# Graph layer with experts: GpSimd splits the expert weights in pieces of 256 columns, padding columns filled behind the first expert's rows

## The chip, the cores and the metric

One core of one Trainium2 chip runs the kernel. The metric is the device time of one execution in microseconds (us), lower is better; three executions are given as their median with the lowest and the highest. One further execution was profiled, and all rows below are from that one.

## What is computed

The reference takes 6250 nodes with 256 features and 206250 edges sorted by target node:

```python
xn = _layernorm(x)
x = x + edge_attention(xn) + mixer(xn)          # graph attention over the edges, and a linear attention
h = _layernorm(x)                               # from here on: the expert part
logits = h @ gate_w + gate_b                    # 8 experts
idx = argmax(softmax(logits)); prb = its probability
C = ceil(1.25 * T / E)                          # 977 rows of capacity for each expert
buf[e, pos] = h                                 # a row goes to its expert's next free slot, if pos < C
hmid = relu(buf @ w1[e] + b1[e])                # 977 x 256 by 256 x 1024
ybuf = hmid @ w2[e] + b2[e]                     # 977 x 1024 by 1024 x 256
x = x + ybuf[idx, pos] * prb * kept
```

All of it is in 32-bit floats.

## The kernel before

The first 2,706 us of the profiled execution are the edge attention and the mixer, which the change leaves alone. Then come the second layer norm with the routing, and the experts.

**Routing** (lines 1380 to 1590). The rows go by in seven groups of seven tiles. VectorE takes the statistics, ScalarE the square root and the centering, TensorE the transposes and the gate's product, VectorE the argmax and the slots (`route`), and GpSimd scatters each tile of rows into the DRAM buffer `hb_d` with one indirect DMA (L1473, 49 of them). Before these scatters GpSimd's queue holds `split_w(0, 0)`, the split of the first expert's `w1`.

**Splitting.** TensorE multiplies in a rounded 32-bit form, so every operand x is kept as two parts: `hi`, a copy of x in that form (L1544), and `lo = x - hi` (L1545). A product is then three products: hi by hi, hi by lo, lo by hi (`product`, L129 in the profile). The function `split` writes both parts with whichever engine it is given. VectorE splits the rows after their transposition, straight out of PSUM, 512 columns at a time. GpSimd splits the weights in `split_w(e, i)`: i = 0 is `w1` (128 partitions by 2048 columns), i = 1 is `w2` (the same size), with one copy and one subtraction of 2048 columns each, and a wait between them.

**Experts** (lines 1607 to 1690). For each expert e, in this order on each engine's queue:

- GpSimd: `split_w(e, 1)`, as soon as `w2` is there and the scatters of the expert before are through its queue.
- TensorE, first product: 8 blocks f of 128 hidden columns, each in two column groups of 490 and 488 rows with 6 matmuls for each, 96 in all. ScalarE writes each group twice with bias and ReLU (L1645): to `hf[f % 2]`, a plain copy in one of two buffers, and to `hh`, the hi part. VectorE then writes `hl = hf - hh` over 978 columns (L1647). ScalarE's block f waits for VectorE's block f-2, since `hf` has two buffers.
- TensorE: `turn(e+1, 0)`, the transposes (L1615) of half of the next expert's rows. VectorE splits them (L1544, L1545).
- GpSimd: `split_w(e + 1, 0)`, which waits until the first product of e has read `w1`.
- TensorE, second product: waits for `split_w(e, 1)`. Eight row tiles j, each over the 8 blocks f with 3 matmuls of 256 columns, 192 in all. Block f waits for its L1647. After two pairs of tiles lies `turn(e+1, 1)`.
- For each pair of tiles VectorE adds the bias out of PSUM (L1670), ScalarE scales (L1674), VectorE replaces infinities and NaN (L1678 to L1683), and GpSimd issues two indirect DMAs that add to the output (L1686).

**Padding.** `hh` and `hl` have 1024 columns for each block, of which L1647 and L1645 write 978. The 46 others are zeroed once, ahead of the first `turn(0, 0)`: a memset of `hf[0]` (L1602) and two copies of 368 columns (L1605) into `hh` and `hl`, on VectorE.

```python
        def split_w(e, i):
            w, hi, lo, used = ((w1r, w1h, w1l, t_l1), (w2r, w2h, w2l, t_l2))[i]
            wait(G, t_wl[i][e], used.get(e - 1))
            t_ws[i][e] = split(G, g, hi, lo, w)
...
        t_pad = v(V.memset(hf[0], 0.0))
...
        turn(0, 0)
        turn(0, 1)
```

Of the kernel before, what the change touches and what calls it, by code (L numbers as in the profile page):

```python
# [14 lines left out]
CP = 1024  # L15
CE = 978
# [16 lines left out]
class Sem:  # L33
# [6 lines left out]
    def inc(self, ins, k=1):  # L40
        ins.then_inc(self.h, k)
        self.n += k
        return (self, self.n)
# [19 lines left out]
def gps_layer_kernel(nc, x, src, dst, wall, ball, wmix, wqm, wout, wo, bo, b_out, gate_w, gate_b, w1, b1, w2, b2, out):  # L63
    f32 = mybir.dt.float32
# [4 lines left out]
    ALU = mybir.AluOpType  # L69
    ACT = mybir.ActivationFunctionType  # L70
    AX = mybir.AxisListType
    V, S, T, G, Y = nc.vector, nc.scalar, nc.tensor, nc.gpsimd, nc.sync

    ctx = ExitStack()
    with ctx:
# [15 lines left out]
        def take(n):  # L91
            top[0] += n
            assert top[0] <= 53008 - WIDE, top[0]
            return A[:, top[0] - n:top[0]]

        def r3(ap, b):
            return ap.rearrange("p (a b) -> p a b", b=b)
# [14 lines left out]
        wait = Waits()  # L112

        def v(ins):
            return sv.inc(ins)

        def a(ins):
            return sa.inc(ins)

        def g(ins):  # L120
            return sg.inc(ins)
# [4 lines left out]
        def product(o, pairs, first=True, last=True):  # L126

            for i, (l, r) in enumerate(pairs):
                m = T.matmul(o, l, r, start=(first and i == 0), stop=(last and i == len(pairs) - 1))  # L129
            return m  # L130


        R0 = take(12544)
# [164 lines left out]
        def norm(xt, n, o=None):  # L298
# [4 lines left out]
            for i in range(n):  # L303
# [8 lines left out]
        quot, hi, lo, over = [R1[:, 16 * i:16 * i + NB13] for i in range(4)]  # L312
# [5 lines left out]
        t = v(V.tensor_copy(firsts, fi_i))  # L318
        wait(V, t)
        t = v(V.tensor_scalar(out=quot, in0=firsts, scalar1=0.5, scalar2=1.0 / NT, op0=ALU.add, op1=ALU.mult))  # L320
        wait(V, t)
        t = v(V.tensor_copy(hi_i, quot))
        wait(V, t)
        t = v(V.tensor_copy(hi, hi_i))
        wait(V, t)
        t = v(V.tensor_tensor(over, hi, quot, ALU.is_gt))
        wait(V, t)
        t = v(V.tensor_tensor(hi, hi, over, ALU.subtract))
        wait(V, t)
        t = v(V.scalar_tensor_tensor(out=lo, in0=hi, scalar=-float(NT), in1=firsts, op0=ALU.mult, op1=ALU.add))  # L330
        v(V.tensor_tensor(oneH, iota.unsqueeze(1).to_broadcast([128, NB13, 128]), hi.unsqueeze(2).to_broadcast([128, NB13, 128]), ALU.is_equal))
        wait(V, t)
        t = v(V.tensor_tensor(oneL, iota[:, 0:NT].unsqueeze(1).to_broadcast([128, NB13, NT]),
                              lo.unsqueeze(2).to_broadcast([128, NB13, NT]), ALU.is_equal))
# [4 lines left out]
        t = v(V.memset(cnt[:, 0:1], 0.0))  # L339
        wait(V, t_hist)  # L340
        t = v(V.tensor_copy(cnt[:, 1:50], ps[5][:, 0:NT]))
        wait(V, t)
        t = v(V.tensor_tensor_scan(R1[:, 1280:1330], cnt, cnt, 0.0, ALU.add, ALU.bypass))
# [3 lines left out]
        t = v(V.tensor_copy(below, ps[5][:, 64:65]))  # L347
# [316 lines left out]
        t = a(S.activation(bh, bal, ACT.Copy))  # L664
# [4 lines left out]
        t = v(V.tensor_scalar(out=bh0, in0=bh.bitcast(f32), scalar1=e0, scalar2=None, op0=ALU.mult))  # L669
# [40 lines left out]
        for grp in range(7):  # L710
            for j in range(7):
                t = grp * 7 + j
# [33 lines left out]
                for u in tiles:  # L746
# [14 lines left out]
                    if 16 <= u < 32:  # L761
                        i = u - 16
# [101 lines left out]
        t = v(V.memset(dsb, 0.0))  # L864
        wait(V, t, t_dt[NT - 1])
        for h in range(4):
            for q in range(2):
                t = v(V.tensor_copy(dsb[q * 64:(q + 1) * 64, h, q * 64:(q + 1) * 64], dts[h][q * 64:(q + 1) * 64, q * 64:(q + 1) * 64]))
# [3 lines left out]
        t = sp.inc(m)  # L872
        wait(V, t)
        for h in range(4):
            t = v(V.tensor_copy(T1[:, h, :], ps[h][:, 0:256]))
# [4 lines left out]
        t = sp.inc(m)  # L880
# [595 lines left out]
        t_sc = [None]  # L1476
# [33 lines left out]
        def out_group(grp):  # L1510
            wait(Y, t_x2[grp])
            if grp < 6:
                return dma(Y, out[grp * 896:(grp + 1) * 896, :].rearrange("(t p) d -> p t d", p=128), XH[:, grp * 7:grp * 7 + 7, 0:256], s_o)
            dma(Y, out[grp * 896:grp * 896 + 768, :].rearrange("(t p) d -> p t d", p=128), XH[:, 42:48, 0:256], s_o)
            return dma(Y, out[48 * 128:N, :], XH[0:N - 48 * 128, 48, 0:256], s_o)
# [5 lines left out]
        w1r, w2r = r3(R0[:, 0:2048], 1024), r3(R0[:, 2048:4096], 256)  # L1521
        b1_s = R0[:, 4096:4160]
        b2_s = R0[:, 4160:6208]
        hf = [R0[:, 6208 + CE * i:6208 + CE * (i + 1)] for i in range(2)]
        yv = [R0[:, o:o + 512] for o in (8192, 8704, 11272, 11784)]
        t_yq = {}
        u1, u2 = R0[:, 9216:9728], R0[:, 9728:10240]
        rowb = [[z.rearrange("p (j w) -> p j w", w=HR) for z in p] for p in
                ((R3[:, 0:1032], R3[:, 1032:2064]), (R0[:, 10240:11272], IDX[:, 0:1032]))]
        hh, hl = [r3(HL[:, 8192 * i:8192 * (i + 1)], 1024) for i in range(2)]  # L1530
        xh, xl = [r3(HL[:, 16384 + 2048 * i:16384 + 2048 * (i + 1)], 1024) for i in range(2)]
        w2h, w2l = [r3(HL[:, 20480 + 2048 * i:20480 + 2048 * (i + 1)], 256) for i in range(2)]
        w1h, w1l = [r3(HL[:, 25344 + 2048 * i:25344 + 2048 * (i + 1)], 1024) for i in range(2)]
        s_we = [sem("s_we0"), sem("s_we1")]
        t_l1, t_l2, t_xp, t_xc, t_y = {}, {}, {}, {}, {}
        t_wl, t_ws = ({}, {}), ({}, {})

        def load_w(e, i):
            wait(Y, t_ws[i].get(e - 1))
            t_wl[i][e] = dma(Y, (w1r, w2r)[i], kpart((w1, w2)[i][e]), s_we[i])  # L1540

        def split(eng, inc, hi, lo, x):

            wait(eng, inc(eng.tensor_copy(hi, x)))  # L1544
            return inc(eng.tensor_tensor(lo, x, hi.bitcast(f32), ALU.subtract))  # L1545

        def split_w(e, i):
            w, hi, lo, used = ((w1r, w1h, w1l, t_l1), (w2r, w2h, w2l, t_l2))[i]
            wait(G, t_wl[i][e], used.get(e - 1))
            t_ws[i][e] = split(G, g, hi, lo, w)  # L1550

        wait(Y, t_fin)
        load_w(0, 0)
        wait(G, t_fin)
        split_w(0, 0)
        t_nm = {0: scale2(0, root2(0, spread2(0)))}
        for s_ in range(NT + 3):
            grp, i = divmod(s_, 7)
            if i == 0 and grp < 7:
                t_o = out_group(grp)  # L1560
# [22 lines left out]
        t_sc = t_sc[0]  # L1583
# [14 lines left out]
        load_w(0, 1)  # L1598
        t_rl = {0: load_r(0), 1: load_r(1)}
        load_w(1, 0)  # L1600
        wait(V, t_sc, t_o)
        t_pad = v(V.memset(hf[0], 0.0))  # L1602
        wait(V, t_pad)
        for z in (hh, hl):
            v(V.tensor_copy(z[:, :, CE:CP], r3(hf[0][:, 0:8 * (CP - CE)], CP - CE)))  # L1605
        bank_free = {}

        def turn(e, jj):

            wait(T, t_rl[e][jj])  # L1610
            for k in range(2):
                b = ps[k]
                wait(T, bank_free.get(k))
                for j in range(4):
                    m = T.transpose(b[:, j * 128:(j + 1) * 128], rowb[e % 2][jj][:, j, k * 128:(k + 1) * 128], ident)  # L1615
                t_xp[e] = sp.inc(m)
                wait(V, t_xp[e], t_l1.get(e - 1))
                bank_free[k] = split(V, v, *[z[:, k, jj * 512:(jj + 1) * 512] for z in (xh, xl)], b[:, :])
            t_xc[e] = bank_free[1]

        COLS = [(0, 490), (490, 488)]
        turn(0, 0)
        turn(0, 1)
        t_hs = {}
        wait(S, t_bb, t_sc, t_o)
        wait(V, t_bb)
        wait(G, t_o, t_sc)
        for e in range(8):
            split_w(e, 1)
            if e > 0 and e + 1 < 8:  # L1630
                load_w(e + 1, 0)
# [4 lines left out]
            for f in range(8):  # L1636
                for n, (c0, cw) in enumerate(COLS):
                    i = 2 + (f * 2 + n) % 4
                    wait(T, bank_free.get(i))
                    fs, cs = slice(f * 128, (f + 1) * 128), slice(c0, c0 + cw)  # L1640
                    t = sp.inc(product(ps[i][:, 0:cw], [(l[:, k, fs], r[:, k, cs]) for k in range(2)
                                                        for l, r in ((w1h, xh), (w1h, xl), (w1l, xh))]))
# [6 lines left out]
            if e + 1 < 8:  # L1649
                turn(e + 1, 0)  # L1650
                split_w(e + 1, 0)
            wait(T, t_ws[1][e])
            for j in range(0, 8, 2):
                rows_ = rowb[e % 2][j // 4]
                jr = j % 4
                i = 6 + j // 2 % 2
# [16 lines left out]
                for jj in (j, j + 1):  # L1673
                    t = a(S.activation(y[:, (jj - j) * 256:(jj - j + 1) * 256], y[:, (jj - j) * 256:(jj - j + 1) * 256], ACT.Copy,  # L1674
                                       scale=rows_[:, jj % 4, 257:258]))
# [3 lines left out]
                t = v(V.tensor_scalar(out=u2, in0=y, scalar1=0.0, scalar2=-1e4, op0=ALU.is_lt, op1=ALU.mult))  # L1679
# [3 lines left out]
                t = v(V.copy_predicated(y, u2.bitcast(i32), u1))  # L1683
# [39 lines left out]
```

## Time and profile before

| | |
|---|---|
| Median of 3 runs | 3256.96 us (3250.91 to 3258.57) |
| Profiled execution | 3256.88 us, of which the span of its records is 3255.3 us |
| VectorE busy | 2563.4 us (79%) |
| TensorE busy | 2218.1 us (68%) |
| GpSimd busy | 2073.9 us (64%) |
| ScalarE busy | 709.9 us (22%) |
| Routing and second norm | 2706 to 2811 us of the span |
| Experts | 2811 to 3254 us of the span |

How to read it: the profile records each instruction with its start, its length, the line of the kernel it comes from and the shapes it wrote and read. PE is TensorE (PEld its loads of weights), DVE VectorE, ACT ScalarE, POOL GpSimd, SP the queue that issues most DMAs. In square brackets stands how long the engine was idle ahead of the instruction, and whose completion ended that. An instruction's length includes time in which it had started and could not proceed. PEclk is the clock granted to TensorE, as a share of 2.4 GHz.

### The profile page before, as it was taken

The numbers are of one execution on the slowest core, as the hardware profiler recorded it, in microseconds if no ns is written. First come the engines' busy times: TensorE is split into PE (matmuls) and PEld (weight loads), VectorE is DVE, ScalarE is ACT, GpSimd is POOL, SyncE is SP. The second block draws the span as 40 slices with busy tenths as digits, with TensorE's granted clock in tenths as the row PEclk, the third lists the DMA queues.
The fourth block names the chain that finished last, engine by engine and source line by source line (L and its number), as shares of the span: only waits on it lengthen the run. The fifth ranks groups of instructions, "written<-read, shape, count | busy, mean of one in ns | idle before, by whom it ended". The sixth has DMA issues, their size and how long they took to land. (4 is left out here: it accounts for less than half of the span.)

```text
span 3255.3 us, 36410 instructions
## 1 busy us (share of the span) xinstructions
PE 2218.1 (68%) x9298; PEld 1743.9 (54%) x9299; DVE 2563.4 (79%) x3578; ACT 709.9 (22%) x2051; POOL 2073.9 (64%) x1996
## 2 busy tenths in 40 slices
PE   6896996778785566555655565655555545698988
PEld 4674775556564444443444443444444425587877
DVE  4555767888899899898989898988989854477675
ACT  3442551111111011111111111111111104434343
POOL 5107605776777777777776777777776774455454
PEclk9998998887888778888788888778888865699999
DMA  6722406887887777777776777777776757223231
GB/s 214 264 100 59 124 27 199 251 241 234 249 239 212 212 213 213 212 211 210 197 200 186 212 212 212 212 211 213 213 205 186 206 66 235 99 68 78 67 81 13
DMA packets 243171, 574.52 MB, mean 176 GB/s; under 512 B 42200, under 2 KB 122001, under 8 KB 242493
## 3 DMA queue, kind: packets, MB, share of 16 engines
q0 software_dynamic: 155184, 465.49, 53.2%
q1 hardware_dynamic: 78170, 95.00, 8.6%
q10 hardware_dynamic: 9296, 9.44, 0.8%
q14 instruction: 480, 3.92, 0.4%
q8 instruction: 41, 0.67, 0.1%
HBM read 504.57 MB, written 70.16 MB: 177 GB/s over the span
## 5 line engine op out<-in xcount | busy, mean ns | idle before, releaser
L1008 POOL DMA_INDIRECT wide<-kv_d,arena x1099 | 1056.6, 961 | 433.9 <-issue 331.1
L1189 PE MATMUL ps<-wide,arena 128*128 128x264 f32 x2432 | 762.0, 480 | 445.4 <-DVE wide L1322 445.3
L1189 PEld LDWEIGHTS ps<-wide,arena 128*128 128x128 f32 x2432 | 573.1, 242 | 631.0 <-DVE wide L1322 498.7
L1008 POOL DMA_INDIRECT arena<-kv_d,arena x539 | 518.5, 962 | 210.9 <-issue 158.1
L1289 DVE TENSOR_REDUCE arena<-arena 128x64 f32<-128x2048 f32 x229 | 523.4, 2286 | 7.9
L1189 PE MATMUL ps<-arena 128*128 128x264 f32 x1216 | 378.5, 478 | 180.0 <-DVE arena L1322 179.9
L1189 PEld LDWEIGHTS ps<-arena 128*128 128x128 f32 x1216 | 284.9, 240 | 271.4 <-DVE arena L1322 208.7
L129 PE MATMUL ps<-halves 128*128 128x256 f32 (+2 forms) x2304 | 379.5, 327 | 34.9 <-DVE halves L1647 30.0
L129 PEld LDWEIGHTS ps<-halves 128*128 128x128 f32 x2304 | 344.6, 200 | 66.0 <-DVE halves L1647 33.2
L1322 DVE TENSOR_TENSOR wide<-wide,ps 128x2112 f32<-128x2112 f32 x152 | 356.8, 2347 | 29.1 <-issue 29.1
L1286 DVE TENSOR_TENSOR arena<-wide,ps 128x2048 f32<-128x2048 f32 x153 | 348.9, 2280 | 10.8 <-DMA wide<-kv_d,arena 10.4
L1111 ACT ACTIVATE ps<-arena 128x64 f32<-128x64 f32 x228 | 51.9, 228 | 1344.4 <-DVE arena L1340 1339.8
L1686 POOL DMA_INDIRECT out<-arena x64 | 107.6, 1681 | 162.8 <-DVE arena L1683 107.9
L1647 DVE TENSOR_TENSOR halves<-arena,halves 128x978 fp32r<-128x978 f32 x64 | 151.9, 2397 | 53.7 <-ACT halves L1645 53.7
L1303 DVE TENSOR_TENSOR arena<-arena,ps 128x264 f32<-128x264 f32 x230 | 97.1, 422 | 118.7 <-issue 116.5
L1108 ACT ACTIVATE ps<-wide 128x256 f32 x228 | 88.4, 388 | 450.1 <-DVE arena L1286 427.3
L1322 DVE TENSOR_TENSOR arena<-arena,ps 128x2112 f32<-128x2112 f32 x76 | 178.4, 2347 | 0.0
L1286 DVE TENSOR_TENSOR arena<-arena,ps 128x2048 f32<-128x2048 f32 x76 | 173.2, 2279 | 0.5 <-ACT ps L1108 0.4
L543 POOL DMA_INDIRECT arena<-src_d,arena x49 | 50.7, 1035 | 169.9 <-issue 169.9
L129 PE MATMUL ps<-mix_halves 128*128 128x512 f32 x392 | 140.0, 419 | 3.7 <-DVE mix_halves L807 3.7
L1156 PE MATMUL ps<-arena 128*128 128x128 f32 x49 | 17.3, 353 | 175.1 <-DVE arena L1279 175.1
L129 PE MATMUL ps<-rear_halves,row_halves 128*128 128x512 f32 (+1 forms) x392 | 128.4, 379 | 0.0
(333 smaller groups left out, 3141.2 us busy)
## 6 DMA issues: line engine op xcount, KB each, us to landing
wide<-kv_d,arena POOLq DMA_INDIRECT x1099, 3.8
arena<-in_w SPq DMA_DIRECT2D x16, 1024.0 KB, 5.3
kv_d<-wide SPq DMA_DIRECT2D x49, 260.0 KB, 2.4
arena<-kv_d,arena POOLq DMA_INDIRECT x539, 3.8
hb_d<-arena SPq DMA_DIRECT2D x16, 516.0 KB, 3.2
arena<-hb_d SPq DMA_DIRECT2D x16, 516.0 KB, 4.7
q_d<-wide SPq DMA_DIRECT2D x49, 128.0 KB, 2.8
xn_d<-arena SPq DMA_DIRECT2D x7, 896.0 KB, 8.4
```

What stands on the lines that cost most here:

```text
L129: m = T.matmul(o, l, r, start=(first and i == 0), stop=(last and i == len(pairs) - 1))
L543: s_ix.inc(G.indirect_dma_start(out=idx0[:, c, :], out_offset=None, in_=src_d, in_offset=bass.IndirectOffsetOnAxis(ap=rpc[:, c:c + 1], axi ...
L1008: e.indirect_dma_start(out=kvb[k][:, j, :], out_offset=None, in_=kv_d, in_offset=bass.IndirectOffsetOnAxis(ap=ixb[k][:, j:j + 1], axis=0)) ...
L1108: e.activation(q_ps, qsf[:, bass.ds(val(e, q_at, NT * 256), 256)], ACT.Copy).then_inc(e_q, 1)
L1111: e.activation(p_ps, Db[:, 0:8 * J], ACT.Exp)
L1189: m = e.matmul(psE[(k + 1) % 3][:, 0:264], ident, kvb[b][:, j, 256:ROW], start=(j == 0), stop=(j == J - 1))
L1286: e.tensor_tensor(prod.rearrange("p (j n) -> p j n", n=256), kvb[k][:, :, 0:256], q_ps.unsqueeze(1).to_broadcast([128, J, 256]), ALU.mult) ...
L1289: e.tensor_reduce(S_ps[:, 0:8 * J], prod.rearrange("p (n d) -> p n d", d=32), AX.X, ALU.add).then_inc(e_red, 1)
L1303: e.tensor_tensor(acc, acc, psE[(k + 1) % 3][:, 0:264], ALU.add).then_inc(e_sc, 1)
L1322: e.tensor_tensor(kvv[b], kvv[b], p3.unsqueeze(3).to_broadcast([128, J, 8, 33]), ALU.mult).then_inc(e_pv, 1)
L1647: t_hs[e * 8 + f] = v(V.tensor_tensor(hl[:, f, 0:CE], hf[f % 2], hh[:, f, 0:CE].bitcast(f32), ALU.subtract))
L1686: t_yq[q] = s_ye[q % 4].inc(G.indirect_dma_start(out=out, out_offset=bass.IndirectOffsetOnAxis(ap=rows_[:, jj % 4, 256:257].bitcast(i32), ...
```

## The change

`split_w` writes both parts in eight pieces of 256 columns, first the eight copies, then, after one wait for the last copy, the eight subtractions. The signal that others wait for comes with the last piece. The operands are the same places in memory, written as flat ranges. The padding (one memset, two copies) moves behind `turn(0, 0)` and `turn(0, 1)`, and takes its zeros from 368 columns of `u1`, a scratch buffer of the output step, in place of `hf[0]`.

```diff
         def split_w(e, i):
-            w, hi, lo, used = ((w1r, w1h, w1l, t_l1), (w2r, w2h, w2l, t_l2))[i]
-            wait(G, t_wl[i][e], used.get(e - 1))
-            t_ws[i][e] = split(G, g, hi, lo, w)
+
+            w, hi, lo = [z[:, o:o + 2048] for z, o in ((R0, 2048 * i), (HL, (25344, 20480)[i]), (HL, (27392, 22528)[i]))]
+            wait(G, t_wl[i][e], (t_l1, t_l2)[i].get(e - 1))
+            for c in range(0, 2048, 256):
+                t = g(G.tensor_copy(hi[:, c:c + 256], w[:, c:c + 256]))
+            wait(G, t)
+            for c in range(0, 2048, 256):
+                t_ws[i][e] = g(G.tensor_tensor(lo[:, c:c + 256], w[:, c:c + 256], hi[:, c:c + 256].bitcast(f32), ALU.subtract))
...
         load_w(1, 0)
-        wait(V, t_sc, t_o)
-        t_pad = v(V.memset(hf[0], 0.0))
-        wait(V, t_pad)
-        for z in (hh, hl):
-            v(V.tensor_copy(z[:, :, CE:CP], r3(hf[0][:, 0:8 * (CP - CE)], CP - CE)))
         bank_free = {}
...
         turn(0, 0)
         turn(0, 1)
+        wait(V, t_sc, t_o)
+        t_pad = v(V.memset(u1[:, 0:8 * (CP - CE)], 0.0))
+        wait(V, t_pad)
+        for z in (hh, hl):
+            v(V.tensor_copy(z[:, :, CE:CP], r3(u1[:, 0:8 * (CP - CE)], CP - CE)))
         t_hs = {}
```

## Rows read from the trace of the kernel before

**Rows 1.** Page, the chain of work that ended last, shares of the span by line.

```profile
PE ps L129 8%; DVE halves L1647 3%; ACT halves L1645 1%; ACT arena L1645 0%; PE ps L1615 0%; DVE halves L1605 0%; POOL hb_d L1473 0%; POOL out L1686 0%; DVE halves L1545 0%; DVE halves L1544 0%; DMA hb_d<-wide,arena 0%; ACT arena L1674 0%; DVE arena L1602 0%; DVE arena L1683 0%; DVE arena L1681 0%
```

**Rows 2.** Waits in the experts, 2806 to 3256 us: total us, times, longest us.

```profile
PE ps L129 <- DVE halves L1647: 30.0, 7, 4.8
```

**Rows 3.** Timeline, expert 1's first product and what follows: start us, us, instruction.

```profile
2880.80 2.49 POOL L1544 CAST halves<-arena 128x2048 fp32r<-128x2048 f32 x1
2881.43 9.49 DVE L1647 TENSOR_TENSOR halves<-arena,halves 128x978 fp32r<-128x978 f32 x3 [1.50 <-ACT halves L1645]
2883.37 5.43 POOL L1545 TENSOR_TENSOR halves<-arena,halves 128x2048 fp32r<-128x2048 f32 x1
...
2894.29 1.90 POOL L1544 CAST halves<-arena 128x2048 fp32r<-128x2048 f32 x1 [5.50 <-PE ps L129]
...
2894.55 8.06 DVE L1647 TENSOR_TENSOR halves<-arena,halves 128x978 fp32r<-128x978 f32 x2 [1.06 <-ACT halves L1645]
...
2896.27 5.31 POOL L1545 TENSOR_TENSOR halves<-arena,halves 128x2048 fp32r<-128x2048 f32 x1
...
2902.67 11.10 PE L129 MATMUL ps<-halves 128*128 128x256 f32 x75 [4.78 <-DVE halves L1647]
```

**Rows 4.** Timeline, expert 0's first product and the start of its second.

```profile
2835.28 1.18 DVE L1647 TENSOR_TENSOR halves<-arena,halves 128x978 fp32r<-128x978 f32 x1 [1.50 <-ACT halves L1645]
...
2847.49 1.90 POOL L1544 CAST halves<-arena 128x2048 fp32r<-128x2048 f32 x1 [29.58 <-PE ps L129]
...
2848.65 1.77 DVE L1647 TENSOR_TENSOR halves<-arena,halves 128x978 fp32r<-128x978 f32 x1 [1.50 <-ACT halves L1645]
...
2850.34 0.68 DVE L1544 CAST halves<-ps 128x512 fp32r<-128x512 f32 x1
```

**Rows 5.** Chain that ended last, in order of time: start us, us, piece, matmuls.

```profile
2848.23 11.51 PE ps L129 x96
2859.73 0.87 PE ps L1615 x8
...
3186.16 0.87 PE ps L1615 x8
...
3224.44 20.79 PE ps L129 x171
```

**Rows 6.** TensorE by stretches: window us, its length, busy us (instructions), PEclk, DMA share, GB/s.

```profile
2900.00:2905.00 5.00, 2.33 (x11) 0.51 0.35 140
...
2910.00:2915.00 5.00, 5.00 (x45) 1.00 0.01 3
```

**Rows 7.** Timeline, the start of the experts.

```profile
2812.48 5.64 DVE L1605 CAST halves<-arena 128x368 fp32r<-128x368 f32 x2
...
2814.88 1.97 PE L1615 MATMUL ps<-arena 128*128 128x128 f32 x8 [18.42 <-DMA arena<-hb_d]
2818.04 0.68 DVE L1544 CAST halves<-ps 128x512 fp32r<-128x512 f32 x1
```

**Rows 8.** Timeline, routing beside the first split.

```profile
2731.89 4.51 POOL L1545 TENSOR_TENSOR halves<-arena,halves 128x2048 fp32r<-128x2048 f32 x1
...
2733.49 2.95 DVE L1497 TENSOR_SCALAR arena<-arena 128x7 f32<-128x7 f32 x1
...
2744.61 1.05 POOL L1473 DMA_INDIRECT hb_d<-wide,arena  x1 [8.20 <-DVE arena L1507]
...
2765.18 0.98 POOL L1473 DMA_INDIRECT hb_d<-wide,arena  x1 [2.71 <-DVE arena L1470]
```

**Rows 9.** Timeline of GpSimd, the start of the kernel.

```profile
0.87 0.20 POOL L187 MEMSET arena<- 128x128 f32 x1 [0.29 <-POOLq L1713]
1.01 0.20 POOL L188 MEMSET arena<- 128x128 f32 x1
...
1.60 0.29 POOL L191 TENSOR_SCALAR_AFFINE_SELECT arena<-arena 128x128 f32<-128x128 f32 x1 [0.24 <-POOL arena L189]
1.84 0.29 POOL L193 TENSOR_SCALAR_AFFINE_SELECT arena<-arena 128x128 f32<-128x128 f32 x1
```

## The prediction

> **What bounds the kernel now.** I read the chain of work that ended last first. Its shares by line [rows 1] name TensorE's products at L129, then VectorE's subtraction L1647, then ScalarE's L1645: in the part where the change lies, TensorE sets the pace and something on VectorE interrupts it. Next I read the waits of the experts: TensorE waited 30.0 us in seven waits, the longest 4.8 us, for L1647 [rows 2]. Then the timeline around one such wait.
>
> Undisturbed, L1647 takes 1.18 us and starts every 2.68 us (1.18 plus 1.50 idle), with TensorE as the pacemaker [rows 4]. In expert 1 three of them take 9.49 us, and later two take 8.06 [rows 3]. The starts and ends show why. GpSimd's copy ends at 2883.29 (2880.80 + 2.49). The first L1647 had started at 2881.43, so it can't have run until then. It and its two successors end at 2890.92; GpSimd's subtraction ends at 2888.80, and from there to 2890.92 is 2.12 us, two of them. So one ran ahead of GpSimd's work, in the gap between copy and subtraction, and the next sat through the whole subtraction. GpSimd paid too: its subtraction took 5.43 us here and 4.51 where no such VectorE instruction cut in [rows 8], so an L1647 costs it 0.92 us. The two engines exclude each other, one whole instruction at a time. A VectorE copy that reads PSUM is not touched: 0.68 us at 2850.34 while GpSimd subtracts [rows 4].
>
> The Trainium skill says the same (SBUF — State Buffer, "Who interferes with whom": a VectorE instruction with two SBUF inputs and a GpSimd instruction that reads SBUF lock each other out for the full instruction). By that rule, the trace agrees, and a shorter GpSimd instruction means a shorter lockout.
>
> What a lockout costs is seen on TensorE. In expert 1 the first one makes L1647 late, so that blocks 6 and 7 are both still open when the split of the next `w1` starts at 2894.29; block 6 gets through after the copy, block 7 only after the subtraction, and TensorE waits 4.78 us for it [rows 3]. Behind that wait its clock is 0.51 of full, the 1.2 GHz level, and it is 1.00 again from 2910 [rows 6]: 75 matmuls take 11.10 us [rows 3] where 96 took 11.51 [rows 5], that is 2.1 us more than their 9.0. Expert 0 has no lockout in its first product, since its `w2` was split before, and there block 7 took 1.77 us and TensorE did not wait [rows 4]. Expert 0 is the picture of what the change aims at.
>
> **The change, part by part.**
>
> Pieces, the gain. The longest lockout falls from a 4.5 us instruction to one piece: 4.51 / 8 = 0.56 us plus a small fixed part, for the copies 1.90 / 8 = 0.24. L1647 then takes at most about 1.8 us of its 2.68, ScalarE is never held up, and block 7 is ready as in expert 0. What an undisturbed expert takes on TensorE: first product 8 blocks x 2.68 = 21.4 [rows 4]; transposes twice 0.87; second product twice 11.51 [rows 5]; sum 46.2 us. What it takes now: from the transposes at 2859.73 to those at 3186.16 are six experts in 326.4 us [rows 5], 54.4 each. Gain 326.4 - 6 x 46.2 = 49.2 us. Of the 8.2 per expert, 4.8 is the wait, 2.1 the clock behind it, and the rest sits in short waits of the first product. Last expert, from 3186.16: now the last matmul ends at 3245.23; undisturbed 0.87 + 11.51 + 21.4 + 192 x 20.79/171 (23.3) = 57.1 gives 3243.3 [rows 5]. Gain 1.9. That stretch also shows that a short wait of TensorE ahead of it did not cost the clock: its 171 matmuls took 0.122 us each, against 0.120 at 1.00.
>
> Pieces, the cost. Fourteen more instructions in each split. Nothing in this trace shows GpSimd's small copies, so bounds from the nearest rows [rows 9]: two memsets of 128 columns start 0.14 us apart and two affine selects 0.24; at the copy's own rate 128 columns are 0.12, so an instruction adds between 0.02 and 0.12 us. I take 0.08, nearer to the affine select, which reads SBUF as the pieces do. A split then takes 1.9 + 0.1 + 4.5 + 14 x 0.08 = 7.6 us of GpSimd's own time (6.8 to 8.2), in place of 6.5. Below zero I exclude: no piece does less per column.
>
> Who waits for that. The split of `w2` stands in front of the second product. In expert 1 it begins at 2883.29 - 1.89 = 2881.4; its first product begins at 2859.73 + 0.87 + 11.5 = 2872.1 [rows 3, 5], so the split starts 9.3 us in, behind the scatters. VectorE now gets its turn every time: five L1647 fall into the split, 0.92 us each, 4.6. End: 9.3 + 7.6 + 4.6 = 21.5 us, while TensorE needs it at 21.4 + 0.87 = 22.3. It fits by 0.8 us. With 0.12 a piece it is 22.1, still in time. If each L1647 shuts GpSimd out for its full 1.18 us, 1.3 us more, and it is late by up to 1.1. In the last expert there are no transposes between, so it is late by 0.1 to 2. I take 0.2 us for each of seven experts, 1.4 us in all, and 7 x 1.5 = 10.5 as the far end. The split of the next `w1` runs beside the second product, 23 us long, with 21 more until it is needed: 1.1 us longer costs nothing. The weight loads behind both splits on SP's queue start about 5 us later and have tens of us of slack. VectorE's L1678 to L1683 on the first pair of tiles may now meet the end of the `w1` split, under 0.6 us each; only scatters wait for them, and they have slack until the last pair.
>
> Routing. The first split stood in the way of L1497, seven columns, 2.95 us where 0.1 to 0.2 is natural for it; it came free at the subtraction's end, 2736.40 [rows 8]. Behind it in VectorE's order are the slots for the first scatters at 2744.61, and through ScalarE the whole pipeline of groups; the second batch of scatters made GpSimd wait 2.71 us at 2765.18 [rows 8], and from there to the end of routing GpSimd scatters without a gap. So the 2.8 us are on the path. With pieces L1497 waits up to 0.6, and a few two-input instructions behind it meet pieces too. I take 2.0 us of gain, bounds 0 and 2.8.
>
> Padding. The two padding copies took 5.64 us, locked out by copy and subtraction of the `w2` split; VectorE began to split the first rows at 2818.04 though TensorE's transposes had begun at 2814.88 [rows 7]. The split reads PSUM, so nothing locks it out. Four cold transposes are half of 1.97 us, so it can begin at about 2815.9: gain 2.1 us, bounds 1 and 2.5. The three instructions now lie in front of the first L1647, which waits some 6 us for ScalarE: under 2 us of work, hidden. Without that cover they'd cost about 1 us. This part works even if the pieces do not.
>
> Sum: 49.2 + 1.9 + 2.0 + 2.1 - 1.4 = 53.8 us. The profiled execution took 3256.88, the median is 3256.96, the same for this purpose. 3256.9 - 53.8 = 3203.
>
> **The rivals.**
>
> A, the new wait. GpSimd's split of `w2`, always giving way, ends after TensorE wants it, by 1 to 2.5 us an expert. It speaks for this that the slack is 0.8 us on a sum of three estimates; against it, that even the upper fixed cost fits. Seven times 1.8 less the 1.4 taken: 3214. A wait as long as 4.8 us would lose the clock too; that takes 0.4 us for each extra instruction, more than any row shows.
>
> B, the pieces don't open the lock, and this is the one that can end slower. GpSimd's memsets start 0.14 us apart though each is recorded with 0.20 [rows 9]: instructions of that engine overlap, so without a wait between them the port may never fall free, and VectorE stays out for all eight copies and then for all eight subtractions. The gap it used until now, at 2883.3, lay where GpSimd waited for its own copy [rows 3]. Then all lockouts remain and each grows with the fixed cost: 7 x 0.08 = 0.6 us on the subtractions and as much on the copies, each on the path once or twice an expert, 1 to 1.7 us, seven times: 7 to 12 slower, less 2.1 for the padding. Time 3262 to 3267, say 3264. It turns slower by more than 0.3% (9.8 us) from about 0.1 us for each instruction. Against it: the other way round, three L1647 in a row let GpSimd in between [rows 3].
>
> The Trainium skill has the rule for B (GPSIMD Engine Reference, "Instruction dispatch": a core starts the next GpSimd instruction as soon as it has done its share of the last, without waiting for completion). Rows 9 agree with it; whether the lock is held across such a boundary no run here shows.
>
> C, GpSimd is starved: where the port changes hands, an extra instruction costs 0.6 us. The split of `w2` then ends 9.3 + 6.5 + 8.4 + 5.5 = 29.7 us in, 7.4 late, and TensorE's clock drops as now, 2.1: 9.5 us lost where 8.2 are lost now, 1.3 more in seven experts, less 4.1 for routing and padding. 3262. No row comes near that price.
>
> **How the numbers follow.** Forecast (in time, or late by under 0.5 us): 0.62. A: 0.22. B: 0.11, of which two thirds within 0.3%. C: 0.03. Something smaller than all, such as a partial opening with half of the gain: 0.02. The range reaches from 3195 (everything at its favourable end: no late split, 2.8 in routing, and as much again from short waits) to 3226 (A at 2.5 us with routing at nothing); B and C stay outside, with 0.14. What a measurement of this kernel can tell from no change is about 0.3%. Faster by over 0.3%: 0.86. Within: 0.08. Slower: 0.06.
>
> **What would show each step.** In the changed kernel's trace: no L1647 longer than 1.9 us (pieces open the lock); TensorE's 7 waits of 4.8 us gone and PEclk 1.00 throughout the experts after the first microseconds; transposes L1615 of neighbouring experts about 46.2 us apart; if they are 47 to 49, the wait in front of the second product names GpSimd (A). L1647 still 4 to 5 us long means B. L1497 beside the first split under 0.8 us, the first scatter about 2 us earlier. The first VectorE split of rows 1 us behind the first transposes. The forecast falls if GpSimd's pieces add over 0.12 us each or if VectorE is shut out across pieces.

## The result, and the profile after

The changed kernel takes 3204.6 us (median of 6 runs, 3200.59 to 3209.64) against 3254.97 of the kernel before (6 runs, 3250.91 to 3258.57): ratio 0.985, 95% interval 0.984 to 0.986. The forecast was 3203, with a range of 3195 to 3226. By the medians the gain is 50.4 us; the forecast had 53.8, from a start of 3256.9.

The span of the profiled execution fell from 3255.3 to 3203.3 us, 52.0 us. The lines below are of the changed kernel. There L1647 is L1652, L1645 is L1650, and GpSimd's copies and subtractions of the weights are L1552 and L1555. First the chain that ended last, by line, which answers to [rows 1].

```profile
PE ps L129 7%; POOL halves L1555 2%; POOL halves L1552 1%; POOL out L1691 1%; PE ps L1615 0%; ACT arena L1679 0%; DVE arena L1688 0%; DVE arena L1686 0%; DVE arena L1675 0%; POOL hb_d L1473 0%; DMA arena<-hb_d 0%; DVE arena L1687 0%; DVE arena L1683 0%; DVE arena L1684 0%; DVE halves L1545 0%
```

VectorE's subtraction was second in this list and is gone from it. In its place stand GpSimd's weight splits and the scatter ahead of them. The waits of the experts, which answer to [rows 2] (who waited for whom: total us, times, longest us):

```profile
PEld ps L129 <- POOL halves L1555: 4.3, 7, 1.6
ACT arena L1650 <- DVE halves L1652: 3.8, 7, 0.9
PE ps L129 <- POOL halves L1555: 2.0, 4, 1.2
```

TensorE's 30.0 us of waiting for VectorE are gone. What is left is a wait for GpSimd in each of the seven experts, 4.3 us in all at the weight loads (PEld), which run ahead of the matmuls; 2.0 us of it show at the matmuls themselves, in four of the seven. Now expert 1, which answers to [rows 3] (timeline: start us, us, instruction):

```profile
2874.74 2.03 POOL L1691 DMA_INDIRECT out<-arena  x1 [0.30 <-issue]
...
2876.19 4.30 POOL L1552 CAST halves<-arena 128x256 fp32r<-128x256 f32 x8
2876.83 4.70 DVE L1652 TENSOR_TENSOR halves<-arena,halves 128x978 fp32r<-128x978 f32 x2 [1.50 <-ACT halves L1650]
...
2880.58 9.27 POOL L1555 TENSOR_TENSOR halves<-arena,halves 128x256 fp32r<-128x256 f32 x8
...
2882.72 1.18 DVE L1652 TENSOR_TENSOR halves<-arena,halves 128x978 fp32r<-128x978 f32 x1 [1.19 <-ACT halves L1650]
...
2884.96 1.27 DVE L1652 TENSOR_TENSOR halves<-arena,halves 128x978 fp32r<-128x978 f32 x1 [1.06 <-ACT halves L1650]
...
2887.52 1.74 DVE L1652 TENSOR_TENSOR halves<-arena,halves 128x978 fp32r<-128x978 f32 x1 [1.29 <-ACT halves L1650]
...
2888.74 1.03 PE L1615 MATMUL ps<-arena 128*128 128x128 f32 x8
...
2889.90 11.77 PE L129 MATMUL ps<-halves 128*128 128x256 f32 x96
```

Two things are to be seen. Among the eight subtractions VectorE gets in at once or within 0.56 us, as forecast. Among the eight copies it does not: of the two L1652 from 2876.83, the first takes 3.42 us, about the longest of the kernel (one line's instructions: min, median, max in ns, below). The same instruction takes 3.4 us in three experts and 2.8 in the other four. And GpSimd's split ends at 2889.85 (2880.58 + 9.27), while TensorE's transposes began at 2888.74: the second product starts only with GpSimd's last piece.

```profile
L1652 DVE TENSOR_TENSOR halves<-arena,halves x64: 1157/1210/3428, 2825.0 to 3170.0; 128x978 fp32r<-128x978 f32 x64
```

TensorE's clock stays at full here (window us, its length, busy us of PE, PEld, DVE, ACT, POOL, then PEclk):

```profile
2900.00:2950.00 50.00, 49.88 (x335) 46.38 (x335) 34.59 (x45) 22.80 (x40) 37.49 (x41) 1.00 0.36 93
```

The chain gives the distance from one expert to the next, as [rows 5] did:

```profile
2855.12 0.87 PE ps L1615 x8
...
3134.95 0.87 PE ps L1615 x8
```

Six experts in 279.8 us, 46.6 each, against 54.4.

Where the 52.0 us came from, each from the starts of the same instruction in both traces:

| Part | forecast | measured |
|---|---|---|
| Up to the second norm, untouched code | 0 | 1.8 |
| Routing, to the first scatter | 2.0 | 1.5 |
| First scatter to first product | 2.1 | 1.9 |
| First product of expert 0 | 0 | -0.6 |
| Six experts | 49.2 less 1.2 | 46.6 |
| Last stretch | 1.9 less 0.2 | 0.8 |
| Sum | 53.8 | 52.0 |

The 1.8 us ahead of the routing are a difference between two executions of the same code, and no gain of the change; without them it is 50.2 us, which agrees with the medians. The loss in expert 0's first product is TensorE's clock. The product starts earlier, at 2818.34 in place of 2823.50. PEclk is 0.50 from 2815 to 2820 and 0.56 from 2820 to 2825, where before it was 0.50 to 2825 and 0.66 from there to 2830; behind that it is 1.00 in both. By an estimate from these shares about 6.1 us of the product ran at the 1.2 GHz level, 4.9 before. Its 96 matmuls took 24.41 us where they had taken 23.85.

### The profile page after: what moved, and what is told of

The parts are those of the page before. It is cut to its first block and busy times, and to the rows that moved or that the text cites. A ratio compares the mean times of both kernels' runs of the same rounds, so it can differ in the third digit from the quotient of the medians.

```text
span 3203.3 us, 36634 instructions
## 1 busy us (share of the span) xinstructions
PE 2197.0 (69%) x9298; PEld 1727.7 (54%) x9299; DVE 2506.5 (78%) x3578; ACT 713.3 (22%) x2051; POOL 2132.2 (67%) x2220
## 5 line engine op out<-in xcount | busy, mean ns | idle before, releaser
L1189 PE MATMUL ps<-arena 128*128 128x264 f32 x1216 | 370.9, 471 | 186.5 <-DVE arena L1322 186.5
L129 PE MATMUL ps<-halves 128*128 128x256 f32 (+2 forms) x2304 | 362.1, 319 | 4.0 <-POOL halves L1555 2.0
L129 PEld LDWEIGHTS ps<-halves 128*128 128x128 f32 x2304 | 331.6, 192 | 31.9 <-POOL halves L1555 4.3
L1652 DVE TENSOR_TENSOR halves<-arena,halves 128x978 fp32r<-128x978 f32 x64 | 93.9, 1476 | 69.5 <-ACT halves L1650 69.5
```

The costliest lines, as they stand in the source:

```text
L1189: m = e.matmul(psE[(k + 1) % 3][:, 0:264], ident, kvb[b][:, j, 256:ROW], start=(j == 0), stop=(j == J - 1))
L1652: t_hs[e * 8 + f] = v(V.tensor_tensor(hl[:, f, 0:CE], hf[f % 2], hh[:, f, 0:CE].bitcast(f32), ALU.subtract))
```

## The experiments

The kernels down to the one with a wait after the first copy ran on two other chips, where the kernel before takes 3714 to 3715 us and not 3255; the last three ran on one where it takes 3259. The time is lost ahead of the experts (what for, no run here asks), and an expert takes there what it takes here: the padding-only kernel, whose splits are those of before, shows 53.9 to 54.6 us an expert, as before did. So ratios are given against the kernel before on the same chip, and the reading is done on the distance between the transposes of neighbouring experts, which repeats to 0.2 us.

### Padding alone

```diff
-            for c in range(0, 2048, 256):
+            for c in range(0, 2048, 2048):
```

(both loops, with pieces of 2048)

> Padding moved, splits whole as before. Theory (the padding copies are locked out by the w2 split and hold up the first VectorE split): from the first transposes L1615 to the first product it is 6.6 us as in the changed kernel, where before it was 8.6, everything else as before: six experts in 326 us, span about 2 us under before. Rival (the start is bound by the row loads or TensorE's cold transposes): 8.6 us stays.

Measured: ratio 0.9998 (0.9987 to 1.0008). From the first transposes at 3293.43 to the first product at 3300.06 it is 6.6 us, against 8.6 before (from 2814.88 [rows 7] to 2823.50). The mechanism is as expected and its 2 us can't be seen in the time. This kernel also writes its operands as flat ranges, like the changed one, and its undisturbed whole copy and subtraction take 1.89 and 4.51 us as before: the new way of writing them brings nothing.

### Pieces alone

```diff
+        wait(V, t_sc, t_o)
+        t_pad = v(V.memset(hf[0], 0.0))
+        wait(V, t_pad)
+        for z in (hh, hl):
+            v(V.tensor_copy(z[:, :, CE:CP], r3(hf[0][:, 0:8 * (CP - CE)], CP - CE)))
         bank_free = {}
```

(the padding back in its old place)

> Pieces of 256, padding ahead of the first rows as before. Theory: six experts in 280 us, the first scatter as in the changed kernel. The padding copies now meet pieces, so part of their 5.64 us goes too: if the lock opens at each piece they take about 1.5 us in all and the start is as fast as in the changed kernel (6.6 us); if eight copies in a row keep the lock, about 3 us and the start is 7.5 us or more.

Measured: ratio 0.9866 (0.9846 to 0.9886), 46.6 to 46.8 us an expert. The start (timeline):

```profile
3266.72 3.05 POOL L1552 CAST halves<-arena 128x256 fp32r<-128x256 f32 x8 [1.39 <-issue]
...
3267.77 1.05 DVE L1610 CAST halves<-arena 128x368 fp32r<-128x368 f32 x2
...
3270.14 1.97 PE L1620 MATMUL ps<-arena 128*128 128x128 f32 x8 [16.19 <-DMA arena<-hb_d]
```

The two padding copies take 1.05 us beside GpSimd's pieces, where they took 5.64 beside whole instructions [rows 7]. They are over before the transposes begin, and the first product again comes 6.6 us behind them. So moving the padding brings 2 us alone and nothing on top of the pieces: the forecast's 2.1 for it was right in size, and either half of the change earns it.

### Pieces for w1 alone, pieces for w2 alone

```diff
-            for c in range(0, 2048, 256):
+            n = 256 if i == 0 else 2048
+            for c in range(0, 2048, n):
```

(both loops, with pieces of `n`; for `w2` alone the condition is `i == 1`)

> Only the w1 splits in pieces, the w2 splits whole. Theory (TensorE's 4.8 us wait needs both lockouts, the w2 one to make L1652 late and the w1 one to catch blocks 6 and 7): the wait shrinks to about 1 us, no drop of the clock, 48.3 us an expert, time 3213 to 3218. Rival (each lockout costs its own half): 50.5 us an expert, 3229.

> Only the w2 splits in pieces, the w1 splits whole. Theory: L1652 stays on its beat, so only block 7 meets the whole copy of w1 (1.9 us) and TensorE waits 0.5 us for it: 47.0 us an expert, time 3207 to 3212. Rival (each lockout costs its own half): 50.5 us an expert, 3229.

Measured: 47.6 us an expert with `w1` alone, less than the 48.3 expected, ratio 0.9889 (0.9871 to 0.9906); 46.9 to 47.1 with `w2` alone, ratio 0.9871 (0.9847 to 0.9895). The first of the two, in its expert 1 (timeline):

```profile
3331.36 9.50 DVE L1653 TENSOR_TENSOR halves<-arena,halves 128x978 fp32r<-128x978 f32 x3 [1.50 <-ACT halves L1651]
...
3344.71 2.75 PE L129 MATMUL ps<-halves 128*128 128x256 f32 x21
...
3348.03 9.26 PE L129 MATMUL ps<-halves 128*128 128x256 f32 x75 [0.57 <-DVE halves L1653]
```

The long lockout in the first product is all there, 9.50 us for three L1653 as before, and yet TensorE waits 0.57 us and not 4.78, and the 75 matmuls behind take 9.26 us and not 11.10. So a lockout in the first product costs 1.5 us an expert by itself (47.6 against the 46.16 of the next kernel). That the buffers between TensorE and VectorE, `hf` and the four PSUM banks of the first product, take up the rest is my reading of the code; no run here changes their number. Taking away either of the two lockouts takes away nearly all of the loss, 6.8 and 7.4 of 7.8 us an expert, which rules out that each had its own half.

### No splits at all

The weights of experts 1 to 7 are not split; the products use the first expert's parts.

```diff
+            if e > 0:
+                wait(G, (sg, sg.n))
+                t_ws[i][e] = g(G.memset(rss[0][0:1, 0:1], 0.0))
+                return
```

> Leaves work out: the weights of experts 1 to 7 are not split, one tiny GpSimd memset stands in for each split, and the products use the first expert's parts. The rest as in the changed kernel. It shows what TensorE's work takes with neither lockout nor a wait for GpSimd: 46.1 to 46.2 us an expert by the sum of the prediction, no L1652 over 1.3 us. If it is 46.5, the rest of the changed kernel's period isn't GpSimd's.

Measured: 46.16 us an expert, six times over, L1656 (the subtraction) never above 1.18 us. So the forecast's 46.2 was TensorE's own work, and each of the changed kernel's six distances, 46.5 to 46.7, holds 0.4 to 0.6 us of waiting for GpSimd.

### Pieces of 512

```diff
-            for c in range(0, 2048, 256):
+            for c in range(0, 2048, 512):
```

(both loops and all slices)

> All splits in four pieces of 512, padding moved. Own time of a split by the changed kernel's rows (0.136 us for each extra instruction) 6.5 + 6 x 0.136 = 7.3 us in place of 8.4, so the w2 split ends 21.2 us into the first product, 1.1 before TensorE needs it. Theory (in the changed kernel this wait is what is left): TensorE waits for GpSimd no more, 46.2 to 46.3 us an expert in place of 46.6, last stretch 1 us shorter, 3 to 4 us under the changed kernel. L1652 up to 2.4 us. Rival (the longer pieces make VectorE late again): waits of TensorE for L1652 come back, 47 us or more.

Measured: ratio 0.9859 (0.9837 to 0.9881), to be read beside the changed kernel's below; 46.16 us an expert, the same as with no splits. The first part of the second product, in expert 1, and L1652 over the kernel (one line's instructions: min, median, max in ns):

```profile
3352.11 1.04 PE L1615 MATMUL ps<-arena 128*128 128x128 f32 x8
3352.91 11.75 PE L129 MATMUL ps<-halves 128*128 128x256 f32 x96
```

```profile
L1652 DVE TENSOR_TENSOR halves<-arena,halves x64: 1162/1536/2318, 3288.8 to 3630.5; 128x978 fp32r<-128x978 f32 x64
```

There is no idle time in brackets ahead of the second product. L1652 is slower than in the changed kernel on the median and still under its beat of 2.68 us, so nobody waits for it. From the first transposes to the end of the span it is 386.3 us, against 390.6 in the changed kernel on the same chip. This is the better kernel by the traces, by some 4 us; the times of the runs can't tell the two apart.

### The changed kernel again

Unchanged, on the chip of the kernels with no splits, with pieces of 512 and with one wait.

> The changed kernel itself, beside the others on one chip, to compare with. Expert period 46.6 us, as in its first profile.

Measured: ratio 0.9872 (0.9847 to 0.9897), 46.5 to 46.7 us an expert, longest L1652 3427 ns where the first profile had 3428.

### One wait after the first copy

```diff
             for c in range(0, 2048, 256):
                 t = g(G.tensor_copy(hi[:, c:c + 256], w[:, c:c + 256]))
+                if c == 0:
+                    wait(G, t)
```

> Pieces of 256, with one more wait of GpSimd for its own first copy before the second. In the changed kernel one L1652 of each expert takes 2.8 to 3.4 us in the copies of w2, which start while the scatter before them still runs for 0.6 us, that is with GpSimd's cores out of step. Theory (out of step, some core always holds the port, so it doesn't open at the boundaries): after one common wait the cores are in step and the longest L1652 falls to 1.8 us or less. Rival (copies in a row never let a two-input instruction in, in step or not): it stays at 2.5 us or more.

Measured (one line's instructions):

```profile
L1654 DVE TENSOR_TENSOR halves<-arena,halves x64: 1153/1194/1551, 3275.1 to 3620.1; 128x978 fp32r<-128x978 f32 x64
```

The longest fell from 3427 to 1551 ns. 46.7 us an expert: the matmuls wait for GpSimd in all seven experts (2.9 us in all) and not in four. So the long subtraction of the changed kernel costs no time. Where it takes 3.4 us, GpSimd's split of `w2` takes 13.7 us and the expert 46.5 to 46.6; where it takes 2.8, they take 13.8 and 46.7. That fits the new order of things: TensorE now waits for GpSimd, and no longer for VectorE.

### A memset ahead of the split

```diff
+            if e > 0:
+                wait(G, (sg, sg.n))
+                wait(G, g(G.memset(rss[0][0:1, 0:1], 0.0)))
```

> The changed kernel with a GpSimd memset of one element, waited for, ahead of each split of experts 1 to 7; no wait among the copies. If the long L1652 in the copies of w2 comes from GpSimd's cores being out of step after the scatter, it is gone here (1.8 us or less) though the copies run without a pause. If what let VectorE in was only the pause between first and second copy, it stays at 2.8 to 3.4 us.

Measured: 46.8 us an expert, longest subtraction (L1655) 1670 ns. Expert 2 (timeline):

```profile
2920.91 2.03 POOL L1694 DMA_INDIRECT out<-arena  x1 [0.30 <-issue]
2922.36 0.62 POOL L1553 MEMSET arena<- 1x1 f32 x1
2923.00 1.18 DVE L1655 TENSOR_TENSOR halves<-arena,halves 128x978 fp32r<-128x978 f32 x1 [1.49 <-ACT halves L1653]
2923.04 4.76 POOL L1555 CAST halves<-arena 128x256 fp32r<-128x256 f32 x8
...
2925.67 1.18 DVE L1655 TENSOR_TENSOR halves<-arena,halves 128x978 fp32r<-128x978 f32 x1 [1.50 <-ACT halves L1653]
```

The memset of one element is recorded with 0.62 us, from before the scatter's end (2922.94) to just behind it: other memsets of this kernel that take in so little last 0.09 us. By these records part of GpSimd had reached it while another part still worked on the scatter. The copies behind it run without a pause among them, and the L1655 that falls in their middle, at 2925.67, is not held up at all. That is for cores out of step as the cause of the 3.42 us, and against the thought that copies in a row keep VectorE out as such. The first L1655 falls into the pause that the memset's wait makes, so for that one the two can't be told apart.

The changed kernel's own trace has a case without any wait: the `w1` copies of expert 1, which follow GpSimd's subtractions and not a scatter (timeline).

```profile
2889.79 3.76 POOL L1552 CAST halves<-arena 128x256 fp32r<-128x256 f32 x8
2890.20 1.36 DVE L1652 TENSOR_TENSOR halves<-arena,halves 128x978 fp32r<-128x978 f32 x1 [0.94 <-ACT halves L1650]
2890.48 1.35 POOL L1552 CAST halves<-arena 128x256 fp32r<-128x256 f32 x1
```

L1652 gets in after two copies and takes 1.36 us; the third copy, from 2890.48, waits for it. These copies are recorded with 0.40 us each when nothing holds them up, and start 0.34 to 0.35 apart. Behind the scatter the copies start as close together and are recorded with 0.96 to 0.99 us each, so there they overlap by about 0.6 us. Copies in a row without a pause do let VectorE in.

### Pieces of 128 and of 1024

```diff
-            for c in range(0, 2048, 256):
+            for c in range(0, 2048, 128):
```

(and 1024)

> Pieces of 128, 32 instructions a split. Theory (0.136 us for each extra instruction, 0.92 for each L1652): 6.5 + 30 x 0.136 = 10.6 us, the w2 split ends 25.4 us into the first product, TensorE waits 3.1 us for GpSimd: 49.3 us an expert if its clock holds, 51.4 if it drops behind that wait as it did behind the 4.8 us one. Rival (the fixed cost hides in the streaming of small pieces): 46.6 to 47.5.

> Pieces of 1024, 4 instructions a split. Own time 6.5 + 2 x 0.136 = 6.8 us, so no wait for GpSimd. A lockout by a subtraction lasts up to 2.3 us, L1652 up to 3.5, over its beat of 2.68: VectorE falls a little behind and has 1.5 us a beat to catch up. Theory (what counts is whether blocks 6 and 7 are late when the second product wants them): under 0.5 us of wait, 46.2 to 46.7 us an expert. Rival (any lockout over the beat reaches TensorE): 48 us or more.

Pieces of 128: ratio 0.9943 (0.9919 to 0.9967), 51.0 to 51.2 us an expert. Expert 1 and the clock behind its wait:

```profile
2887.08 1.04 PE L1615 MATMUL ps<-arena 128*128 128x128 f32 x8
...
2891.41 13.03 PE L129 MATMUL ps<-halves 128*128 128x256 f32 x96 [3.29 <-POOL halves L1555]
```

```profile
2892.00:2897.00 5.00, 5.00 (x35) 0.77 0.63 211
```

GpSimd's split ends 25.6 us into the first product, 25.4 expected. TensorE waits 3.29 us, and its clock drops behind that: 96 matmuls in 13.03 us and not 11.77, 1.3 more, where the 4.8 us wait cost 2.1 in the kernel before. Well over half of the change's gain is gone.

Pieces of 1024: ratio 0.9849 (0.9820 to 0.9877), 47.2 us an expert, longest L1652 3380 ns; TensorE waits for VectorE again, 0.8 us in the second product. That lies between my two expectations, nearer to the theory's: four L1652 in a row took 10.7 us, VectorE was still late when block 7 was wanted.

| Pieces | us an expert | TensorE waits for |
|---|---|---|
| 2048 (before) | 54.4 | VectorE |
| 1024 | 47.2 | VectorE |
| 512 | 46.16 | nobody |
| 256 (the change) | 46.6 | GpSimd |
| 128 | 51.1 | GpSimd |
| no splits | 46.16 | nobody |

The order of the table rests on these distances. By the ratios alone, 1024, 512 and 256 columns can't be told apart.

## Why the prediction was right, point by point

**The lockouts as the cause: right.** With either of the two opened, TensorE's 4.8 us wait shrinks to under 1 us, and with both it is gone. The explanation that it takes the two together, the first to make L1647 late and the second to catch blocks 6 and 7, is shown by the two half kernels.

**TensorE's own time, 46.2 us: right.** The kernel with no splits has 46.16. The clock part was right too: PEclk is 1.00 through the experts from 2825 on, and in the kernel with `w1` pieces alone the matmuls behind a 0.57 us wait are at full speed.

**The number 3203: in part luck.** The gain was 53.8 us by the forecast and 50.4 by the medians, and the time still came within 1.6 us because the six runs of the kernel before have their median at 3254.97 and not at the 3256.9 that the forecast started from. The bounds of the range don't follow from their terms either: A at 2.5 us with routing at nothing gives 3203 + (7 x 2.5 - 1.4) + 2.0 = 3221 and not 3226, and the favourable end 3203 - 1.4 - 0.8 - 2.8, some 3198, and not 3195. The measured time lies within both.

**The fixed cost of a piece: mis-sized.** The forecast took 0.08 us, with 0.12 as the upper bound, from memsets and affine selects [rows 9]. The first `w2` split, which no VectorE instruction disturbs, shows it (timeline):

```profile
2808.13 2.81 POOL L1552 CAST halves<-arena 128x256 fp32r<-128x256 f32 x8 [1.39 <-issue]
...
2811.02 5.51 POOL L1555 TENSOR_TENSOR halves<-arena,halves 128x256 fp32r<-128x256 f32 x8
```

From 2808.13 to 2816.53 are 8.4 us, where the whole instructions took 6.5; 1.9 over 14 is 0.136 us. Each kind has seven instructions more: copies pay (2.81 - 1.90)/7 = 0.13 us, subtractions (5.51 - 4.51)/7 = 0.14. Pieces of 128 give the same, 10.59 us for the whole split, 4.1 over 30. So the two kinds hardly differ, and the upper bound of 0.12, from instructions of other kinds, was too low for both.

**The late split: rival A came true in part.** With 8.4 us the sum of the forecast gives 9.3 + 8.4 + 4.6 = 22.3 us for the end, just what TensorE has. Measured: start 2876.77 - 2867.5 = 9.3, then 13.1 us, of which five L1652 at 0.92 are 4.6. The forecast put 0.2 us on each expert; the six show 0.4 to 0.6 and the last 1.2, where nothing lies between the products. With that the six experts gave 46.6 us and not 48.0. It was the right sum with one term too small. The wait is the one that A names, but only the last expert's reaches A's 1 to 2.5 us.

**No L1647 over 1.9 us: wrong.** The longest is 3.43. Rival B was half right: the lock can stay closed across pieces, and it does so in the copies behind a scatter, though not in subtractions, in copies behind a wait or behind subtractions, or against the padding copies. It had the price wrong. The long lockout comes once an expert, in the first product, where the kernel with `w1` alone shows that even whole instructions cost only 1.5 us.

The rule of the Trainium skill that stood beside B (GPSIMD Engine Reference, "Instruction dispatch": a core goes on to the next instruction when its own share is done) agrees with the records here: eight copies start 0.34 us apart from 2876.19, the first two of them before the end of the scatter, 2876.77. The same page's "When to use GPSIMD" says that a pair of the eight cores writes a DMA's descriptors. These two would then be late and the other six ahead, which is my conclusion and not the page's. By that, one wait ahead of the copies mends it, and both kernels with a wait agree: 1.55 and 1.67 us.

**Routing: right in kind, 1.5 us and not 2.0.** L1497 is not held up. From the third group's statistics to the first scatter it was 14.15 us (2730.46 to 2744.61) and is 12.67 (2728.66 to 2741.33). The pieces meet later instructions with two inputs, as the forecast had allowed (timeline):

```profile
2731.68 0.17 DVE L1497 TENSOR_SCALAR arena<-arena 128x7 f32<-128x7 f32 x1
...
2732.41 0.86 DVE L1428 TENSOR_TENSOR arena<-arena 128x112 f32<-128x112 f32 x1
...
2735.26 0.26 DVE L1443 TENSOR_TENSOR arena<-arena 128x112 f32<-128x112 f32 x1
2735.55 0.68 DVE L1444 TENSOR_TENSOR arena<-arena 128x112 f32<-128x112 f32 x1
```

L1428 and L1444 take 0.86 and 0.68 us where the like of them, L1443, takes 0.26.

**Padding: right as a step, and superfluous.** 2.0 us measured from the first transposes to the first product (6.64 and 8.62), 2.1 forecast; the pieces earn the same 2 us without it. The forecast said that the padding works without the pieces, and did not ask whether it adds anything to them.

**What was not tried:** whether it is the two descriptor cores that are late. No run here looks at single cores.

## What to carry to other kernels

A long GpSimd instruction that reads SBUF holds up VectorE instructions with two SBUF inputs for its whole length; cut it so that a piece and the VectorE instruction together stay under the beat of the engine that sets the pace. Then count what the cuts add to GpSimd's own time, and look for who waits for its last piece: 0.14 us a piece, and 0.9 us for every VectorE instruction let in, made 512 columns the best here by the traces, and pieces of 128 lost well over half of the gain. When two lockouts catch the same instruction stream, price them together: removing either one may bring almost all.

## What the runs showed of the hardware that was not expected

- GpSimd can keep a VectorE subtraction of two SBUF inputs out over several copies that start 0.34 us apart (3.42 us for a 1.18 us subtraction, let in behind the seventh copy) when the copies follow an indirect DMA directly; with a wait ahead of them or after the first, no subtraction takes over 1.67, and behind GpSimd's own subtractions one takes 1.36.
- An extra GpSimd instruction in a row costs 0.13 us as a copy and 0.14 as a subtraction of two inputs.
- TensorE's clock stayed at the 2.4 GHz level behind waits of 0.3 to 1.2 us, and was at the 1.2 GHz level for a part of the time behind waits of 3.3 us (1.3 us lost) and 4.8 us (2.1 us lost).
- On two other chips the kernel before took 3714 and 3715 us in place of 3255. In the kernels profiled there the difference lies ahead of the experts; its cause is open.
